# Involution: two accumulating transfers in place of GpSimd's join and one VectorE addition

## What is computed

```python
x = x + _L1_conv_ref(_ln_c(x), w_v, w1, gn_gamma, gn_beta, w2, b2)

def _L1_conv_ref(x, ...):
    t = relu(group_norm(d4_1x1(x, w1), gn_gamma, gn_beta, cmid))
    wgt = einsum('oi,bighw->boghw', w2, t) + b2      # for each pixel a 3x3 kernel
    ...                                              # turned for each of 8 orientations
    xv = d4_1x1(x, w_v)
    pats = unfold_patches(xv, 3)                     # the 9 shifted images
    out = (wv * pats).sum(axis=4)                    # sum of 9 products
```

## Time and profile before

| | us |
|---|---|
| median of 3 runs (lowest to highest) | 1269.37 (1269.09 to 1271.05) |
| the profiled execution | 1271.14 |
| its span, first to last instruction | 1269.3 |
| mean granted TensorE clock | 0.922 of full |

### The profile page before, as it was taken

How to read it: one execution, slowest core, us unless ns; L and a number is a source line. 1 busy time by engine, 2 the same in 40 slices (tenths; PEclk the granted TensorE clock), 3 DMA queues, 4 the chain that set the end, 5 groups by cost and what they waited for, 6 DMA issues and landing times. The chain is left out here.

```text
span 1269.3 us, 34850 instructions
## 1 busy us (share of the span) xinstructions
PE 1077.3 (85%) x9969; PEld 731.1 (58%) x9970; DVE 911.5 (72%) x2119; ACT 797.3 (63%) x2044; POOL 550.3 (43%) x402
## 2 busy tenths in 40 slices
PE   6869979988209999999999999668999999965698
PEld 2324435554109999999999999623334433422464
DVE  2662348767826888888878878628999999983587
ACT  5865569998405777777777777546566665622465
POOL 0000006757752333333333333327999999991000
PEclk9989989999558999999999999869999999985599
DMA  6200001451431111111111111130112221102000
GB/s 195 80 1 0 0 1 43 133 173 53 91 56 45 45 42 46 41 44 42 43 45 43 43 44 43 34 92 17 34 49 66 66 66 36 48 34 84 0 2 34
DMA packets 60527, 65.25 MB, mean 51 GB/s; under 512 B 9841, under 2 KB 50301, under 8 KB 60336
## 3 DMA queue, kind: packets, MB, share of 16 engines
q1 hardware_dynamic: 49616, 46.47, 12.9%
q0 software_dynamic: 8832, 17.00, 4.2%
q10 hardware_dynamic: 2016, 0.94, 0.6%
HBM read 37.12 MB, written 28.55 MB: 52 GB/s over the span
## 5 line engine op out<-in xcount | busy, mean ns | idle before, releaser
L933 ACT ACTIVATE m_hh<-ps 128x256 f16<-128x256 f32 x584 | 224.3, 384 | 118.2 <-PE ps L890 88.6
L833 POOL DMA_INDIRECT expert_out<-m_result,m_token x148 | 145.5, 983 | 305.3 <-DVE m_result L989 299.2
L970 DVE SCALAR_TENSOR_TENSOR m_hl<-ps,m_hh 128x256 f16<-128x256 f32 x584 | 241.6, 422 | 44.4 <-ACT m_hh L933 35.3
L870 PE MATMUL ps<-m_x,weights 128*128 128x128 f16 x1168 | 212.9, 220 | 3.5 <-DVE m_hl L970 2.6
L871 PE MATMUL ps<-m_x,weights 128*128 128x128 f16 x1168 | 212.8, 220 | 0.0
L874 PE MATMUL ps<-m_x,weights 128*128 128x128 f16 x1168 | 212.8, 220 | 0.0
L888 PE MATMUL ps<-weights,m_hh 128*128 128x128 f16 x1160 | 210.0, 219 | 0.0
L889 PE MATMUL ps<-weights,m_hh 128*128 128x128 f16 x1160 | 209.9, 219 | 0.0
L890 PE MATMUL ps<-weights,m_hl 128*128 128x128 f16 x1160 | 209.9, 219 | 0.0
L776 POOL DMA_INDIRECT dispatched<-d_rows,slot x128 | 130.2, 1017 | 154.3 <-DVE slot L684 108.0
L1098 POOL TENSOR_TENSOR iv_pool_sum<-iv_pool_sum,iv_pool_part 128x1024 f32<-128x1024 f32 x80 | 188.7, 2359 | 11.7 <-DVE iv_pool_part L1313 3.8
(11 more groups left out here) (305 smaller groups left out, 2299.9 us busy)
## 6 DMA issues: line engine op xcount, KB each, us to landing
m_rows<-dispatched SPq DMA_DIRECT2D x152, 65.5 KB, 1.8
X<-x SPq DMA_DIRECT2D x16, 512.0 KB, 4.4
iv_got<-expert_out SPq DMA_DIRECT2D x16, 512.0 KB, 4.3
out<-X SPq DMA_DIRECT2D x16, 512.0 KB, 3.1
Y<-w_moe SPq DMA_DIRECT2D x8, 512.0 KB
expert_out<-m_result,m_token POOLq DMA_INDIRECT x148, 2.3
dispatched<-d_rows,slot POOLq DMA_INDIRECT x128, 2.6
Y<-w_last SPq DMA_DIRECT2D x1, 2048.0 KB
```

Of the source, the lines that this page charges most:

```text
L833: pool.indirect_dma_start(env.yt, bass.IndirectOffsetOnAxis(ap=token[:, k:k + 1], axis=0), result[:, k, :], None, bounds_check=TOKENS - 1, ...
L870: pe.matmul(out, high, xh, start=True, stop=False)
L933: act.activation(hh[e][:, part_cols[h]], hidden[e][h], ACT.Relu).then_inc(hi_ready[e], 1)
L970: dve.scalar_tensor_tensor(hl[e][:, cols], hidden[e][h], 0.0, hh[e][:, cols], ALU.max, ALU.subtract).then_inc(h_split[e], 1)
```

## The change

GpSimd's join and VectorE's second own addition fall away. X, which already holds the residual, is no longer an input of an engine's addition: GpSimd issues two transfers SBUF to SBUF of 512 KB that add `pool_sum` and then `own_sum` to X (`accum_op=ALU.add`). Tap 6 moves from VectorE's own taps to GpSimd's (`POOL_TAPS` 7, with a seventh `pool_part`), so GpSimd sums seven products with six additions, and VectorE adds its products 7 and 8 once. The transfer of `own_sum` of image n-1 is issued after the first addition of image n, when the transfer of `pool_sum` of image n-1 has landed; SyncE's store waits for the landing of `own_sum`.

```diff
-POOL_TAPS = 6
-OWN_ADDS = TAPS - POOL_TAPS - 1
+POOL_TAPS = 7
+POOL_ADDS, OWN_ADDS = POOL_TAPS - 1, TAPS - POOL_TAPS - 1
...
             def send(n):
-                sp.wait_ge(S["done"], n + 3)
+                sp.wait_ge(S["own_joined"], n * 16 + 16)
...
-            def join(n, q):
+            def join_pool(n, q):
+                wait_apart(pool, S["pool_summed"], n * POOL_ADDS + POOL_ADDS, env.passed)
+                pool.dma_start(image(X, n), flat(pool_sum[q]), accum_op=ALU.add).then_inc(S["pool_joined"], 16)
+
+            def join_own(n, q):
                 pool.wait_ge(S["summed"], n * OWN_ADDS + OWN_ADDS)
-                wait_apart(pool, S["pool_summed"], n * POOL_TAPS + 2 * POOL_TAPS, env.passed)
-                pool.tensor_tensor(grid(image(X, n)), own_sum[q][:, :, :], pool_sum[q][:, :, :], ALU.add).then_inc(S["done"], 1)
+                wait_apart(pool, S["pool_joined"], n * 16 + 16, env.passed)
+                pool.dma_start(image(X, n), flat(own_sum[q]), accum_op=ALU.add).then_inc(S["own_joined"], 16)
 
             def body(n, q, ahead):
-                if not isinstance(n, int) or n > 0:
-                    join(n - 1, 1 - q)
-                for k in range(POOL_TAPS):
+                for k in range(1, POOL_TAPS):
                     pool.wait_ge(S["product_ready"], n * TAPS + k + 3)
...
+                    if k > 1:
+                        pool.wait_ge(S["pool_summed"], n * POOL_ADDS + k - 1)
+                    pool.tensor_tensor(pool_sum[q][:, :, :], pool_part[0][:, :, :] if k == 1 else pool_sum[q][:, :, :],
                                        pool_part[k][:, :, :], ALU.add).then_inc(S["pool_summed"], 1)
+                    if k == 1 and (not isinstance(n, int) or n > 0):
+                        join_own(n - 1, 1 - q)
+                join_pool(n, q)
 
             images(pool, body)
-            join(IMAGES - 1, (IMAGES - 1) % 2)
+            join_own(IMAGES - 1, (IMAGES - 1) % 2)
...
             def tap(n, q, k):
                 if k == 0:
                     pe.wait_ge(S["split_ready"], n + 2)
-                if k < 2 and (not isinstance(n, int) or n > 0):
-                    pe.wait_ge(S["summed"], n * OWN_ADDS + k - 1)
+                if k == 1 and (not isinstance(n, int) or n > 0):
+                    pe.wait_ge(S["summed"], n * OWN_ADDS)
...
                 if k < POOL_TAPS:
-                    dve.wait_ge(S["pool_summed"], n * POOL_TAPS + k + 1)
+                    if not isinstance(n, int) or n > 0:
+                        dve.wait_ge(S["pool_summed"], n * POOL_ADDS - POOL_ADDS + max(k, 1))
...
             def add_pair(n, q):
 
                 dve.wait_ge(S["product_ready"], n * TAPS + POOL_TAPS + 4)
-                dve.wait_ge(S["done"], n + 1)
+                if not isinstance(n, int) or n > 1:
+                    dve.wait_ge(S["own_joined"], n * 16 - 16)
                 dve.tensor_tensor(own_sum[q][:, :, :], grid(tap_out(q, POOL_TAPS + 1)[:, :]), own_part[:, :, :], ALU.add).then_inc(S["summed"], 1)
-
-            def add_last(n, q):
-                dve.wait_ge(S["product_ready"], n * TAPS + POOL_TAPS + 5)
-                dve.wait_ge(S["summed"], n * OWN_ADDS + 1)
-                dve.tensor_tensor(own_sum[q][:, :, :], grid(tap_out(q, TAPS - 1)[:, :]), own_sum[q][:, :, :], ALU.add).then_inc(S["summed"], 1)
...
-                    if k == POOL_TAPS + 1:
-                        add_pair(n, q)
+                    if k == 7:
                         for h in range(2):
                             if ahead >= 2:
                                 norm(n + 2, h)
-                add_last(n, q)
+                add_pair(n, q)
```

More of the change, by code:

```diff
@@ L1001, in phase_involution @@
                  "padded_ready e2_ready group_ready group_taken gvar_ready gln_ready grstd_ready gain_ready coef_ready "
-                 "tf_ready relu_ready split_ready tap_ready product_ready summed pool_summed done w_loaded w_ready border sent").split()
+                 "tf_ready relu_ready split_ready tap_ready product_ready summed pool_summed pool_joined own_joined w_loaded w_ready border sent").split()
         S = {n: ctx.enter_context(nc.semaphore(f"iv_{n}")) for n in names}
@@ L1081, in _ @@
             pool.wait_ge(S["w_ready"], 3)
-            pool.sem_inc(S["pool_summed"], POOL_TAPS)
-            def join(n, q):
+            flat = lambda x: x[:, :, :].rearrange("p h w -> p (h w)")
+            def join_pool(n, q):
+                wait_apart(pool, S["pool_summed"], n * POOL_ADDS + POOL_ADDS, env.passed)
+                pool.dma_start(image(X, n), flat(pool_sum[q]), accum_op=ALU.add).then_inc(S["pool_joined"], 16)
+            def join_own(n, q):
                 pool.wait_ge(S["summed"], n * OWN_ADDS + OWN_ADDS)
-                wait_apart(pool, S["pool_summed"], n * POOL_TAPS + 2 * POOL_TAPS, env.passed)
-                pool.tensor_tensor(grid(image(X, n)), own_sum[q][:, :, :], pool_sum[q][:, :, :], ALU.add).then_inc(S["done"], 1)
+                wait_apart(pool, S["pool_joined"], n * 16 + 16, env.passed)
+                pool.dma_start(image(X, n), flat(own_sum[q]), accum_op=ALU.add).then_inc(S["own_joined"], 16)
             def body(n, q, ahead):
-                if not isinstance(n, int) or n > 0:
-                    join(n - 1, 1 - q)
-                for k in range(POOL_TAPS):
+                for k in range(1, POOL_TAPS):
                     pool.wait_ge(S["product_ready"], n * TAPS + k + 3)
[L1094 to L1098, removed]
+                    if k > 1:
+                        pool.wait_ge(S["pool_summed"], n * POOL_ADDS + k - 1)
+                    pool.tensor_tensor(pool_sum[q][:, :, :], pool_part[0][:, :, :] if k == 1 else pool_sum[q][:, :, :],
                                        pool_part[k][:, :, :], ALU.add).then_inc(S["pool_summed"], 1)
+                    if k == 1 and (not isinstance(n, int) or n > 0):
+                        join_own(n - 1, 1 - q)
+                join_pool(n, q)
             images(pool, body)
-            join(IMAGES - 1, (IMAGES - 1) % 2)
+            join_own(IMAGES - 1, (IMAGES - 1) % 2)
         @block.tensor
@@ L1284, in _ @@
             dve.sem_inc(S["split_ready"], 1)
-            dve.sem_inc(S["done"], 2)
             dve.sem_inc(S["product_ready"], 2)
```

## The result

The changed kernel takes 1298.62 us in the median of four runs (1294.93 to 1300.42), the kernel before 1269.23 (1269.0 to 1271.05, four runs): a ratio of **1.0225, 95% interval 1.02 to 1.025**. It is slower, by 29.4 us. The forecast was 1290.0 in a range of 1264 to 1318, with 0.69 on slower. Each ratio further down is to the kernel before as timed beside that run (median 1270.03 us for runs 1 to 4, 1269.67 for runs 5 to 8). One execution of run 7's kernel took 2751.45 us and one of the kernel before beside it 3813.48, where all others of the two took 1262 to 1274; the ratios leave both out.

A forecast was written before the change was run, and what follows sets the result against it. GpSimd was to become the involution's bound: fourteen periods of 18.6 us against 17.80 gave 11 us, mostly two uncovered end transfers the rest of +20.6, so 1290.0 us, range 1264 to 1318.

The forecast's parts named there:

- Which engine: In the involution, GpSimd becomes the bound: 18.6 us an image against 17.80, waiting for pool_sum's landing after one addition.
- The landing: Accumulating transfer, issue start to landing: 3.83 us if the second read is hidden, 5.72 if doubled; middle 4.8 taken.
- The period: GpSimd, one pool_sum issue to the next: landing L plus 13.8 (gaps, issue 1.28, five additions 12.12), 18.6 us at L 4.8.
- Head, steady state, end: Involution stage: first looped issue at 896.9, fourteen periods of 18.6, 13.0 us of uncovered landings and store; +20.6 us.
- VectorE and TensorE's floor: Involution with a free GpSimd: VectorE 16.45 us an image, TensorE 16.99 through ScalarE's second exponential, so 17.0 us.
- Covered: Rival: the transfer lands under one GpSimd addition (at most 3.64 us), period 17.44, 1271.5 us, no change; chance 0.14.
- Faster by a cheap issue: Rival: GpSimd's issue costs 0.66 us and landing 3.2, TensorE's 17.0 then decides, 1262.5 us; chance 0.17.
- side case of a short issue alone: GpSimd's issue is short but landing L is 4.2 us: period 17.4, stage end +1.4 us.
- SyncE's load: Load of image n+2, queued behind a store waiting for own_sum's landing: more than a whole image of slack, costed at nothing.
- The signs in the profile: GpSimd idle about 1.3 us after addition 1; VectorE idle some 2 us an image, released by GpSimd's additions.

The follow-up runs named there:

- run 7: run 1's kernel, last image finished by VectorE, which also adds products 5 and 6 there, leaving GpSimd four additions: 1265.98 us, ratio 0.9972.
- run 1: Changed kernel with the wait for pool_sum's landing and the issue of own_sum after the next image's second addition instead of its first: 1273.62 us, ratio 1.0035.
- run 4: Changed kernel with accum_op=ALU.add left out, so both transfers copy instead of adding (residual and pool_sum lost from the result): 1271.23 us in one run.
- run 5: run 1's kernel without ScalarE's exponential in the norm: period 16.91 us; 1262.99 us in one run, not to be compared since later stages get other data.
- run 2: Changed kernel with SyncE's load of an image queued one store further ahead, so not behind a store waiting for own_sum: 1295.61 us, ratio 1.0202.
- runs 6 and 7: run 1's kernel with the last image finished by VectorE, adding own_sum and pool_sum to X: 1268.41 us; run 7 also shares out its products: 1265.98 us.

## Why the prediction was right, step by step

- **Which engine.** GpSimd was to become the bound through the wait behind the covering addition, and it did; run 1 removes that wait and gives back 25 of the 29 us, 21.2 of them in the stage.
- **The landing**, 4.8 from 3.83 to 5.72: measured 4.6, by 1.42 + 2.77 + 0.41, where I had 1.55 + 2.83 + 0.39. That the middle hit is luck. The choice was between hidden and doubled, and run 4 shows it doubled (1.92 times); by my rows that would have been 5.72. It came out at 4.6 because the stretch that is doubled was too long in my rows: a copy issued by GpSimd within SBUF moves its bytes in 1.44 us and not in 1.89 as a store to HBM does, and they start 1.12 us after the issue and not 1.55 as a scatter's. So the lower bound was wrong too: the copy lands in 2.9 us. The Trainium skill's fit, page "DMA: Bandwidth & Descriptors", section "Anatomy of one DMA — SWDGE (gpsimd) path", gives an estimate of 3.2 us, nearer to this copy than my rows, but 1.4 too low for the adding transfer. The estimate by both pages of the Trainium skill together, 4.4, is as near to 4.6 as my 4.8. It makes the sum 6.4 us shorter (fourteen periods and two landings by 0.4), not about 7.
- **The period**, 18.6 as L + 13.8: measured 18.90, and 18.93 over the 14 periods from 897.49 to 1162.49. The terms are off in both directions. An issue with its gap is 0.60 us, not 1.28, since GpSimd starts the next addition before the issue's row ends; that addition then takes 2.65 instead of 2.36. Ahead of each issue that follows an addition stand 0.68 us, not 0.2, and about 0.6 instead of 0.2 between a landing and the issue that waits for it. Measured terms: 4.6 + 0.6 + 0.6 + 12.41 + 0.68 = 18.9. That the sum is only 0.3 us off is in part luck: the issue was 0.7 us and the landing 0.2 too dear, the two gaps 0.9 and the additions 0.3 too cheap.
- **Head, steady state, end**, +20.6 us: the stage grew by 24.8. The first issue that the sum stands on came at 897.49 (896.9 said), the fourteen periods took 265.0 (261.7 said), the end 12.69 (13.0 said); the remainder is that the stage began 0.5 us earlier. So the steady state is the term that was too small, by 3.3 us. A further 4.6 us of the medians' 29.4 are not in the stage as profiled: the profiled execution of before was the longest of its runs, that of the change the shortest. Where those 4.6 us are in the other executions stays open.
- **VectorE and TensorE's floor**, 17.0: 17.5 in run 1. The step that named it, ScalarE's second exponential, was right (run 5); its size was read from a trace in which VectorE was late for it, and was 0.5 us too low. It doesn't bear on the change, where GpSimd was later still, but it leaves 0.3 us of the 0.8 an image that any mending of it could give.
- **Covered**, 1271.5 us: run 4 is this rival, with other data. 1271.2 us, the stage 2.1 us longer than before where 2.1 was said, by a gain of some 0.3 us an image and the longer end. It is one execution, and the agreement is partly luck: with its landing of 2.9 us GpSimd's own path is 17.01 us (932.64 to 949.65) and not the rival's 17.44, and what makes 17.49 of it is the wait for VectorE.
- **Faster by a cheap issue**: the issue is cheap, 0.60. Its other half, a landing of 3.2, isn't there for an adding transfer. The side case of a short issue alone (L = 4.2) was added up wrong: its own terms give +0.4, or +1.7 with the 1.3 for the images behind the loop, and not +1.4.
- **SyncE's load**, costed at nothing: it did come late, by up to 2.4 us, and cost nothing (run 2). The cover that I named, a whole image of slack, was wrong, since GpSimd is a whole image behind; what covers it is that TensorE itself waits for GpSimd.
- **The signs in the profile**: GpSimd's idle was to be 1.3 us an image and is 1.97, by the gap behind the landing. VectorE's idle is 2.0 us an image as said (169.1 busy of 189.1 us from 897.49 to 1086.63), but in the loop it does not end with GpSimd's additions (0.4 us in all): it ends with ScalarE's reciprocal roots (9.2) and with TensorE, which waits for the load.

## What to carry to other kernels

A transfer that takes over an engine's addition can pay only where its landing is covered: count the work that stands between the issue and the first wait for it, and put the wait behind at least the landing time (here 4.6 us, two additions and not one, for 21 us of the stage). Cover alone did not make it pay here: run 1 is still 0.35% slower than before. Then look at the last round of the loop, where nothing is left to cover with, and finish it on an idle engine. And before taking work from an engine, find what is next behind it: VectorE was given 1.35 us an image here, and 0.3 of them could be had, since the path through ScalarE (17.5 us) and GpSimd (16.9) stood right behind.

## What the runs showed of the hardware

- An adding transfer of 512 KB within SBUF keeps the DMA engines busy for 2.77 us, a copy for 1.44; from issue to landing 4.6 and 2.9 us.
- GpSimd's issue of the adding transfer has a row of 0.86 us, of the copy 0.56. The next instruction starts 0.60 and 0.58 us after its start, and an addition that starts 0.60 us after the longer one takes 2.65 us, against 2.38 after the shorter and 2.36 away from an issue.
- Additions with both operands in SBUF took longer on VectorE and GpSimd at once, in the last image of runs 6 and 7: 1.52, 1.79 and 3.24 us on VectorE against 1.23 alone, 3.15 us on GpSimd against 2.36. No run was made to part this from other causes.
